# Mixture-of-experts stage: VectorE makes the low parts of the expert weights, and the second expert's are made at one of four places

## The reference

```python
logits = xf @ gate_W.T                       # 4096 tokens, 8 experts
pi = _sinkhorn(-logits)                      # 20 iterations
_, top_idx = jax.lax.top_k(pi, TOP_K)        # two experts for each token
g = jnp.einsum('nd,efd->enf', xf, W_gate)    # D=256, F=1024
u = jnp.einsum('nd,efd->enf', xf, W_up)
y = jnp.einsum('enf,edf->end', jax.nn.silu(g) * u, W_down)
for k in range(TOP_K):
    out = out + y[top_idx[:, k], n_ar] * pi[:, k:k + 1]
```

## Time and profile before

| | before |
|---|---|
| runs, us | 2277.14, 2267.01, 2270.15 (median 2270.15) |
| the profiled execution, us | 2268.48 |
| its span in the profile, us | 2266.9 |
| TensorE matmul busy | 1930.9 us, 85% of the span |
| VectorE busy | 1335.8 us, 59% |
| ScalarE busy | 1381.1 us, 61% |
| GpSimd busy | 806.4 us, 36% |
| mean granted TensorE clock | 0.922 of full speed |

### The profile page before, as it was taken

How to read it: one execution, slowest core, us unless ns; L and a number is a source line. 1 busy time by engine, 2 the same in 40 slices (tenths; PEclk the granted TensorE clock), 3 DMA queues, 4 the chain that set the end, 5 groups by cost and what they waited for, 6 DMA issues and landing times.

```text
span 2266.9 us, 37849 instructions
## 1 busy us (share of the span) xinstructions
PE 1930.9 (85%) x11671; PEld 1096.2 (48%) x11671; DVE 1335.8 (59%) x2199; ACT 1381.1 (61%) x1586; POOL 806.4 (36%) x712
## 2 busy tenths in 40 slices
PE   6899999999665497977878778695989999999998
PEld 5722333333424486866766667574742222222245
DVE  4501145456577355444444454443869999999977
ACT  5699999999433122322223222222779999999944
POOL 2011011011201323234132332311128888888932
PEclk9999999999755798988989889897989999999999
DMA  6644344433104544443434434445983535243121
GB/s 204 214 92 66 57 84 84 84 85 85 39 0 170 186 149 158 141 149 122 169 117 171 149 117 172 140 140 191 333 211 57 133 57 133 47 115 70 29 84 67
DMA packets 131069, 276.06 MB, mean 122 GB/s; under 512 B 18588, under 2 KB 69022, under 8 KB 129656
## 3 DMA queue, kind: packets, MB, share of 16 engines
q1 hardware_dynamic: 117160, 228.72, 36.8%
q0 software_dynamic: 6960, 21.77, 3.0%
q10 hardware_dynamic: 6736, 22.94, 2.7%
HBM read 365.58 MB, written 96.21 MB: 204 GB/s over the span
## 4 chain that ended last, share of the span: by engine, by line
PE 29%; ACT 19%; issue 19%; POOLq 16%; DVE 9%; POOL 5%; DMA 3%; ACTq 1%; SPq 0%; DVEq 0%
PE psum L1345 12%; POOLq L2434 10%; PE psum L1326 9%; ACT A1f_probs L1370 8%; ACT A1f_probs L1378 8%; POOLq L2350 5%; POOL e_x L2404 3%; PE psum L381 2%; PE psum L2615 2%; PE psum L850 1%; DMA qk_parts<-L_part 1%; DVE e_hT L2555 1%; PE psum L396 1%; DMA hidden<-e_squares 1%; ACT f_xn L2890 1%
## 5 line engine op out<-in xcount | busy, mean ns | idle before, releaser
L1326 PE MATMUL psum<-A_qa,A_ka 50*128 50x512 f32 x2048 | 408.5, 467 | 22.9 <-DVE A_qa L1413 6.1
L1326 PEld LDWEIGHTS psum<-A_qa,A_ka 50*128 50x128 f32 x2048 | 176.5, 185 | 470.7 <-DVE A1f_probs L1423 243.3
L2615 PE MATMUL psum<-e_w_high,e_hT 128*128 x1136 | 253.0, 315 | 167.5 <-DVE e_hT L2555 160.5
L2615 PE MATMUL psum<-e_w_high,e_xT 128*128 x1136 | 386.3, 403 | 1.9 <-DVE e_xT L2545 1.7
L1547 POOL TENSOR_TENSOR A1f_probs<-A1f_probs,A1f_bias 128x512 f32<-128x512 f32 x256 | 327.5, 1291 | 83.1 <-ACT A1f_probs L1378 82.7
L1423 DVE SCALAR_TENSOR_TENSOR A1f_probs<-psum,A1f_bias 128x1024 f32<-128x1024 f32 x256 | 311.7, 1218 | 23.7 <-PE psum L1326 20.4
L2489 ACT ACTIVATE e_y<-psum 128x256 f32<-128x256 f32 x71 | 27.3, 385 | 482.0 <-PE psum L2615 244.2
L1378 ACT ACTIVATE A0f_probs<-psum 128x1024 f32<-128x1024 f32 x256 | 314.1, 1227 | 0.0
L1366 ACT ACTIVATE A0f_probs<-psum 128x1024 f32<-128x1024 f32 x256 | 312.2, 1219 | 2.5 <-PE psum L1326 2.4
L2615 PEld LDWEIGHTS psum<-e_w_high,e_hT 128*128 128x128 f32 x1136 | 209.3, 220 | 187.1 <-issue 185.9
L1345 PE MATMUL psum<-A1f_probs,v 128*32 128x512 f32 x2048 | 273.9, 606 | 17.5 <-POOL A1f_probs L1547 16.0
(11 more groups left out here) (297 smaller groups left out, 2637.3 us busy)
## 6 DMA issues: line engine op xcount, KB each, us to landing
e_w_raw<-in_experts ACTq DMA_DIRECT2D x67, 3072.0 KB
hidden<-e_squares SPq DMA_DIRECT2D x69, 512.0 KB, 2.9
e_turned<-hidden SPq DMA_DIRECT2D x276, 128.0 KB, 2.7
qk_parts<-L_part SPq DMA_DIRECT2D x64, 512.0 KB, 4.2
A_qa<-qk_parts SPq DMA_DIRECT2D x192, 128.0 KB, 4.3
A_ka<-qk_parts SPq DMA_DIRECT2D x192, 128.0 KB, 6.4
om<-results SPq DMA_DIRECT2D x16, 512.0 KB, 7.7
e_w_raw<-in_experts SPq DMA_DIRECT2D x2, 3072.0 KB, 11.6
```

What stands on the lines that cost most here:

```text
L1326: mm = e.matmul(ps[:, side * HALF:(side + 1) * HALF], self.qk.ka[rows, s, pair, kt * P:(kt + 1) * P].bitcast(FP32R), self.qk.qa[rows, s, p ...
L2615: mm = e.matmul(out, left[part].bitcast(FP32R), moving.bitcast(FP32R), start=start and i == 0, stop=stop and i == 2)
```

## The change

The low parts move from GpSimd's program to VectorE's, and the place where the second expert's parts are made is chosen among four (start of iterations 1, 2 and 3, or end of iteration 3) in place of two. The core of the diff:

```diff
+    REST = 4
...
+    def if_second(self, e, k):
+
+        before = [self.planned(e, IS_NEW, i) for i in range(1, min(k + 1, self.REST))]
+        total = before[0]
+        for i, is_new in enumerate(before[1:], 2):
+            if i < k or k == self.REST:
+                total = total + is_new
+        if k == 1:
+            return e.If(before[0] > 0)
+        return e.If(total < 1) if k == self.REST else e.If(before[-1] > total)
...
     def pool(self, e):
-        def low_of(buf, a, b):
-        def low_second(j):
-        def low_part(j, a, b, value):
+        def fetch_fourth(k):
+            with self.if_second(e, k):
+                e.wait_ge(self.low_ready, self.low_value("second", k))
                 self.fetch(e, 0, FOURTH, 0, self.fourth_in)
-            e.drain().then_inc(self.low_ready, 1)
...
         for j in range(MOE_TILES):
-            if j in (1, 2):
-                low_second(j)
+            if 1 <= j < self.REST:
+                fetch_fourth(j)
             if j + ROW_BUFS < MOE_TILES:
                 self.load_rows(e, j + ROW_BUFS)
             if j >= self.LAG:
                 self.store_y(e, j - self.LAG)
-            if j >= 1:
-                low_part(j, 0, DOWN_AT, self.up_ready(j))
-            if j >= self.LAG:
-                low_part(j - 1, DOWN_AT, WIDE, self.down_ready(j - 1))
+            if j + 1 == self.REST:
+                fetch_fourth(self.REST)
...
     def act(self, e):
         def high_part(j, a, b):
-            buf = bass.ds(self.planned(e, OTHER_BUFFER, j), 1)
-            is_new = self.planned(e, IS_NEW, j)
-            with e.If(is_new > 0):
+            with e.If(self.planned(e, IS_NEW, j) > 0):
                 e.wait_ge(self.weights_in, DMA * min(max(1, j - 1), MOE_TILES - 1 - self.LAG))
                 if j >= 2:
                     e.wait_ge(self.fourth_in, DMA)
-                high_of(buf, a, b)
+                high_of(bass.ds(self.planned(e, OTHER_BUFFER, j), 1), a, b)
             e.drain().then_inc(self.high_ready, 1)
         def fetch_fourth(j):
-            e.wait_ge(self.low_ready, self.down_ready(j))
+            e.wait_ge(self.low_ready, self.low_value("down", j))
...
-            if j in (1, 2):
+            if 1 <= j < self.REST:
                 high_second(j)
...
                 high_part(j - 1, DOWN_AT, WIDE)
+            if j + 1 == self.REST:
+                high_second(self.REST)
...
     def dve(self, e, beside):
+        def low_second(k):
+            with self.if_second(e, k):
+                e.wait_ge(self.high_ready, self.high_value("second", k))
+                low_of(slice(0, 1), 0, WIDE)
+            e.drain().then_inc(self.low_ready, 1)
+        def low_part(j, kind, a, b):
+            with e.If(self.planned(e, IS_NEW, j) > 0):
+                e.wait_ge(self.high_ready, self.high_value(kind, j))
+                low_of(bass.ds(self.planned(e, OTHER_BUFFER, j), 1), a, b)
+            e.drain().then_inc(self.low_ready, 1)
...
         for j in range(MOE_TILES):
+            if 1 <= j < self.REST:
+                low_second(j)
             if j + 1 < MOE_TILES:
                 split_rows(j + 1)
             if j >= self.LAG:
                 rest_of_hidden(j - self.LAG)
+            if j > self.LAG:
+                low_part(j - self.LAG, "down", DOWN_AT, WIDE)
             multiply(j)
             if j < self.BY_PE:
                 square(j)
+            if j:
+                low_part(j, "up", 0, DOWN_AT)
+            if j + 1 == self.REST:
+                low_second(self.REST)
             if j >= 8:
                 next(beside, None)
+        low_part(MOE_TILES - 2, "down", DOWN_AT, WIDE)
```

More of the change, by code:

```diff
@@ L2350, in planned, with high_value, low_value @@
         return e.value_load(self.plan[0:1, row, j:j + 1], min_val=0, max_val=most)
[L2352 to L2360, removed]
+    def high_value(self, kind, j):
+        order = []
+        for k in range(1, MOE_TILES):
+            order += [("second", k)] * (k < self.REST) + [("up", k)] + [("down", k - 1)] * (k > 1)
+            order += [("second", k + 1)] * (k + 1 == self.REST)
+        return order.index((kind, j)) + 1
+    def low_value(self, kind, j):
+        order = []
+        for k in range(1, MOE_TILES):
+            order += [("second", k)] * (k < self.REST) + [("down", k - self.LAG)] * (k > self.LAG) + [("up", k)]
+            order += [("second", k + 1)] * (k + 1 == self.REST)
+        order += [("down", MOE_TILES - 2)]
+        return order.index((kind, j)) + 1
+    def if_second(self, e, k):
[7 more added lines that the diff above has]
+        return e.If(total < 1) if k == self.REST else e.If(before[-1] > total)
     def fetch(self, e, buf, row, j, sem):
@@ L2459, in high_of, with high_second @@
             e.activation(self.w.high[:, buf, a:b].bitcast(FP32R), self.w.raw[:, buf, a:b], ACT.Copy)
-        def high_second(j):
-            is_new = self.planned(e, IS_NEW, 1)
-            with e.If(is_new > 0 if j == 1 else is_new < 1):
+        def high_second(k):
+            with self.if_second(e, k):
                 e.wait_ge(self.second_in, DMA)
@@ L2569, in multiply, with low_of @@
             e.tensor_tensor(out, *parts, ALU.mult).then_inc(self.hidden, 1)
+        def low_of(buf, a, b):
+            e.tensor_tensor(self.w.low[:, buf, a:b].bitcast(FP32R), self.w.raw[:, buf, a:b], self.w.high[:, buf, a:b],
+                            ALU.subtract)
+        def low_second(k):
+            with self.if_second(e, k):
+                e.wait_ge(self.high_ready, self.high_value("second", k))
[6 more added lines that the diff above has]
+            e.drain().then_inc(self.low_ready, 1)
         def square(j):
@@ L2606, in wait_for_weights @@
             with e.If(buffer_of(j) != buffer_of(j - 1)):
-                e.wait_ge(self.low_ready, self.second_ready(min(j, 2)) if j < 4 else self.up_ready(j - 2))
+                e.wait_ge(self.low_ready, self.low_value("up", j - 2) if j > self.REST + 1 else
+                          self.low_value("second", min(j, self.REST)))
                 if j > 1:
                     with e.If(buffer_of(j - 1) != buffer_of(j - 2)):
-                        e.wait_ge(self.low_ready, self.up_ready(j - 1))
+                        e.wait_ge(self.low_ready, self.low_value("up", j - 1))
         def product(j, out, left, at, n, start, stop):
@@ L2654, in down @@
             if j:
-                e.wait_ge(self.low_ready, self.second_ready(1) if j == 1 else self.down_ready(j - 1))
+                e.wait_ge(self.low_ready, self.low_value("second", 1) if j == 1 else self.low_value("down", j - 1))
             if j:
```

10 lines of the change are left out of this document (removed).

## The result

The changed kernel's median is 2201.93 us (2200.71 to 2205.53, four runs) beside 2273.25 us (2267.01 to 2277.14, four runs) of the kernel before: a ratio of 0.9691, 95% interval [0.9663, 0.9719]. It is 71 us faster by the medians, where the prediction said 126. The time lies above the range's upper end of 2186; it is nearest to what rival 1 gives (new tiles stay dear, 2186), and exceeds even that.

What follows compares the result with a forecast made beforehand. Bound: GpSimd's subtractions stalling VectorE and its queue delaying ScalarE. Of 178 us excess, 56 for new tiles and 2 stay, giving 120; with 6 at the start, 126 off 2268.48 is 2142.5, forecast 2144 us, range 2120 to 2186.

Steps and rivals of the forecast that it cites:

- rival 1: New tiles stay dear at 14 us each, squares' way through HBM crossing a 3 MB transfer: 2186 us, chance 0.15.
- rivals 2 and 3: Calm tiles miss 8.61 us by 0.3: 2164, chance 0.09; VectorE's blocks become the bound: 2306, chance 0.06.
- The first wait: At a new tile, TensorE waits 5 us for the hidden values' low part behind VectorE's subtraction.
- The 6.7 us said to be won at `down(0)`: At the stage's start, rest_of_hidden(0) ends at 753.6 where the first down product began at 760.52 before.
- excess 58 us: Time from rest_of_hidden of tile 3 to tile 68 beyond 559.7 us; 178 before, 58 predicted.
- With 0.9 us for register loads and a late transfer I take 8.0 us per new tile: Cost of a new tile, waits and clock loss included: 56 us for seven, bounds 5.0 and 14 us each.
- I put this one down to GpSimd's queue: TensorE's 3.03 us wait two tiles after a new tile, ascribed to GpSimd's long drains delaying ScalarE.
- at 893 that way had been done: Counter to rival 1: the squares' way through HBM was finished then, and ScalarE was late by GpSimd's drain.
- hidden: VectorE's low down part, 2.28 us before multiply, costs nothing because TensorE wants that result only 6 us later.
- Rival 4: Shared port turns round: VectorE's subtractions hold GpSimd's gathers and y stores, at most 55 us, 2200 us, chance 0.03.
- The start: First tiles of the expert stage, with the second expert's parts at iteration 3's end: 6 us won, bounds 1 and 11.

Runs made afterwards that it cites:

- e11: Kernel before with GpSimd's subtractions left out from the third expert on (stale low parts): 2166.41 us, ratio 0.9555.
- e1: Changed kernel without the seven weight transfers that ScalarE starts at new tiles (stale weights): 2145.45 us, ratio 0.9457.
- e2: Kernel before without the seven weight transfers that ScalarE starts at new tiles (stale weights): 2222.37 us, ratio 0.9812.
- e6: Changed kernel with the 3 MB transfers started by SyncE, behind its turned loads, in place of ScalarE: 2267.87 us, ratio 1.0001.
- e9: Changed kernel with VectorE's low down block moved behind multiply and square: 2237.76 us, ratio 0.9855.
- e5: Changed kernel with WEIGHT_RUN 1024 in place of 4096, so packets a quarter the size: 2208.66 us, ratio 0.9734.
- e3: Changed kernel with the second expert's parts at the start or end of iteration 1, REST 2 in place of 4: 2192.67 us, ratio 0.9672.
- e7: Changed kernel with each weight transfer started by SyncE in three 1 MB pieces over three tiles: 2268.60 us, ratio 1.0005.
- e4: Changed kernel with VectorE's low up part cut in two, the up half and split_rows behind the next iteration's rest_of_hidden: 2213.70 us, ratio 0.9757.

## Why the prediction was wrong

**What held.** The steps about the engines did, within a few tenths of a microsecond. `rest_of_hidden` takes 1.22 us everywhere. VectorE's subtractions are 4.42, 2.29 and 6.56 us. Its drain has a median of 0.475 us, its load 0.304; calm tiles stay at 8.6 us (rivals 2 and 3 didn't happen). The first wait was 5.5 to 6.0 us where 5 was said. At the start `down(0)` to `down(3)` began at 753.20, 763.84, 784.25 and 794.77, where the text says or gives 753.6, 763.9, 784.4 and 794.6; the stage itself began 1.0 us earlier in this execution than in that of before. (The 6.7 us said to be won at `down(0)` are 6.9 by the prediction's own figures; measured, 7.3.) That GpSimd's standstill of VectorE was the largest loss is shown by e11 (101 us), and the size of the sum by e1 (excess 58 us, predicted 58, with the luck told there).

**What failed.** The step is "With 0.9 us for register loads and a late transfer I take 8.0 us per new tile". The late transfer alone costs 7.8 us per new tile, by e1 against the change; 7 x 7.8 = 55 us is the whole of the miss in the stage (excess 113 instead of 58). About 5 to 6.5 us of it is TensorE's second wait, the rest its lower clock behind it.

The evidence was in the trace of before, and was read away. The step "I put this one down to GpSimd's queue" stands for the wait two tiles on (e2 keeps it, e1 has none). But there was another of 2.52 us one tile later, and it belongs to the transfer (e2 removes it). And the counter of rival 1, "at 893 that way had been done", looks at one alignment. Before, the squares of 883.23 went out ahead of the transfer of 887.31, and the next ones, at 895.34, 8.0 us behind it: their distance was 4.88 us (4.9 to 6.6 in all seven). After, the squares stand 0.70 us behind it: 9.2 us. Both had moved. Counted from the first `down` behind the first wait, the transfer started 17.0 to 18.8 us later before and 14.9 to 16.3 after, since VectorE's drain frees it and no longer GpSimd's. The squares of three tiles on went out after 12.9 to 14.3 us before and after 15.6 to 16.8 now, since VectorE's low down part stands ahead of `multiply` and `square`. The prediction called that part "hidden": TensorE doesn't wait for `multiply`, but the squares lost their lead over the transfer by it. The change moved a transfer that was half hidden into the worst place, right ahead of the squares. That the two would meet could be worked out beforehand, from ScalarE's and VectorE's new orders, and rival 1 named it. How long the squares would be held at this distance, no row of before showed; the nearest was 4.9 to 6.6 us at a distance of 8.0.

**Rival 1** thus happened by the mechanism that it names, at 16.2 us per new tile and not 14; it had 0.15. Its reason, squares behind a 3 MB transfer, is shown by e1 (takes it away), e6 (another queue order, 13.45 us) and e9 (squares first: no second wait of 5 us left). e5 excludes the packets' size. Rival 4 in its DMA form is there, and no wait of TensorE is put down to it: see the last section. The start won what it should, 5.8 us of 6 (4.8 of them behind the stage's start), but e3 shows that it could have won 7 to 9 more.

**What stays open.** Most of the squares' delay lies ahead of their first packet (4.1 to 4.7 us in all seven cases), while 215 to 285 of the transfer's 768 packets moved; what holds them there, no run tells. The trace's packet records show only that none of them was moving yet. A place for the transfer that delays neither squares nor ScalarE was not found: e6 and e7 brought a wait of their own through the count. Behind tile 68 the changed kernel lost 3 us of the 70 again (730.4 us of span before, 733.6 after). In all traces this part is 728.0 to 730.6 us with GpSimd's subtractions in their old place or left out there, and 731.8 to 738.9 with VectorE's; no experiment looked into it.

One thing was not tried, and both kernels have it. By the code that makes `plan`, the new tile of the nth expert makes the parts of expert n+1 (the next in line), and its transfer fetches expert n+3. With eight experts only the first four of the seven transfers bring weights that anybody uses, and the parts made at the last new tile are used by nobody; the trace shows all seven transfers moving their 768 packets of 4 KB. At 7.8 us each, leaving out the last three would save some 23 us, an estimate from e1.

## What to carry to other kernels

When a change lets an engine run ahead, list the transfers that this engine or its semaphores start, and put their new start times beside every small transfer on the critical path: 512 KB sent 0.7 us behind 3 MB came 6.6 us late, and nothing about the computation showed it. When two waits follow an event, take the causes away one at a time before giving both to one of them. A semaphore that is raised in every iteration makes a rare order an every-tile cost: e9 moved a block that matters at seven tiles and paid at all the others. And ask of every rare transfer whether its data is wanted at all.

## What the runs showed of the hardware

- A transfer of 512 KB (squares, SyncE's queue) behind one of 3 MB (weights, ScalarE's queue): 2.6 us alone, 8.25 to 9.23 us when sent about 0.7 us behind it, 4.9 to 6.6 us when sent 8 us behind it, 13.45 us when sent 0.53 us behind it in the same queue. With packets a quarter as large it was hardly less (8.05 us). The small transfer did not wait for all of the large one. Its first packet came 4.1 to 4.7 us after it was sent, when 215 to 285 of the 768 large packets had gone; its 128 packets then took 3.2 to 3.9 us beside the others (1.2 alone), and it was through with 309 to 388 large ones still to come.
- GpSimd's indirect DMA took 4.03 us beside each of six of VectorE's 4.45 us subtractions, where its median is 0.98. In GpSimd's timeline:

```profile
855.57 4.03 POOL L2425 DMA_INDIRECT e_x<-token_rows,tokens  x1 [0.30 <-issue]
...
869.06 0.98 POOL L2425 DMA_INDIRECT e_x<-token_rows,tokens  x1 [0.30 <-issue]
```

  It starts inside the subtraction and ends 0.86 us behind it (859.60 against 858.74). The Trainium skill (SBUF — State Buffer, section "SBUF: two separate sides") ties such a block of descriptor writing to VectorE's two-port modes; here it comes beside an fp32 subtraction of two SBUF operands, in which the same section sees a lock only against a GpSimd operation that reads SBUF. Whether the reading of `tokens` makes this DMA one, no run here shows. The rows are six tiles ahead, so nobody waits for it.
- How long TensorE waited doesn't tell by itself whether its clock falls. In e11 the `down` behind a wait of 1.76 us (1346.36) took 4.44 us, and those behind 2.67 us (870.90) and 3.12 us (891.77) took 3.12 and 3.13, at a granted clock of 1.00. In e4 one behind 2.71 us took 4.62, at 0.63; the changed kernel's, behind 5.97 us, took 5.47, at 0.51. Of the seven `down` behind e4's shorter first waits, three took 3.12 to 3.17 us and four 4.62 or 4.63. So cutting a wait in half gives the clock's part back at some tiles and not at others.
